# Preparing keys and values: context and integer weights transposed by the DMA engines, and a reordered opening

## The reference

```
k = (context @ Wk).reshape(B, Nk, h, dh)
v = (context @ Wv).reshape(B, Nk, h, dh)
attn = softmax(einsum('bqhd,bkhd->bhqk', q, k) * scale)
out  = einsum('bhqk,bkhd->bqhd', attn, v) @ Wo + bo

x = x + L0_xattn(layernorm(x), context, ...)
x = x + L0_ffn(layernorm(x), w_gate, w_up, w_down)     # int weights / 127
x = x + L1_xattn(layernorm(x), context, ...)
x = x + L1_ffn(layernorm(x), rhs)                      # quantised to int8
```

## Time and profile before

| | |
|---|---|
| median of three runs | 1627.0 us (1626.41 to 1629.02) |
| time of the profiled execution | 1625.34 us |
| span in its trace | 1623.5 us |
| TensorE busy | 1560.3 us (96%) |
| GpSimd busy | 1271.7 us (78%) |
| head | 0 to about 210.7 us |
| body | about 210.7 us to the end |

### The profile page before, as it was taken

One profiled execution on the slowest core, in us unless ns is written; L12 is line 12 of the kernel. 1 busy time (PEld: TensorE's weight loads), 2 busy tenths in 40 slices (PEclk: granted clock), 3 DMA queues, 4 the chain that ended last, 5 costly groups with the idle time before them and its releaser, 6 DMA issues.

```text
span 1623.5 us, 74775 instructions
## 1 busy us (share of the span) xinstructions
PE 1560.3 (96%) x27354; PEld 1446.7 (89%) x27354; DVE 1357.6 (84%) x3519; ACT 1379.5 (85%) x5665; POOL 1271.7 (78%) x1892
## 2 busy tenths in 40 slices
PE   7999978999999999999999999999999999999995
PEld 4555668999999999999999999999999999999994
DVE  5777757888888888888888887888898889888985
ACT  5665678899998998998999988889999999999993
POOL 4200068899999999998999888788999999999994
PEclk9999999999999999999999999999999999999998
DMA  8975689987887777778778989899999889989995
GB/s 253 327 275 223 221 183 175 160 176 173 176 177 178 168 174 182 166 177 176 171 172 179 173 172 161 153 178 197 191 201 198 189 190 200 198 190 190 196 191 104
DMA packets 732250, 305.82 MB, mean 188 GB/s; under 512 B 621424, under 2 KB 717584, under 8 KB 730064
## 3 DMA queue, kind: packets, MB, share of 16 engines
q1 hardware_dynamic: 730272, 297.29, 83.4%
q0 software_dynamic: 1840, 6.82, 1.3%
HBM read 87.72 MB, written 65.54 MB: 94 GB/s over the span
## 4 chain that ended last, share of the span: by engine, by line
PE 36%; POOL 31%; issue 11%; DVE 5%; DMA 2%; ACT 1%; SPq 1%; POOLq 0%; ACTq 0%; DVEq 0%
PE psum L308 27%; POOL pr L1486 9%; POOL p L1493 8%; POOL p L1489 6%; PE psum L1115 5%; POOL rs L368 3%; POOL hT_l L1476 3%; PE psum L306 2%; PE psum L299 2%; DVE oT_l L337 1%; DMA pT<-p 1%; DVE x L1465 1%; POOL y L1514 1%; POOL x_res L1502 1%; DMA x2T<-x 1%
## 5 line engine op out<-in xcount | busy, mean ns | idle before, releaser
L1230 ACT ACTIVATE ex<-psum,nmax 128x77 f32<-128x77 f32 x2048 | 638.0, 335 | 44.4 <-DVE nmax L1347 35.7
L1230 ACT ACTIVATION_READ_ACCUMULATOR ex<-psum,nmax 128x1 f32 x2048 | 443.3, 216 | 0.0
L1493 POOL TENSOR_TENSOR p<-pr,p 128x308 f16<-128x308 f32 x512 | 413.2, 807 | 38.4
L1486 POOL TENSOR_TENSOR pr<-ex,rden 128x308 f32<-128x308 f32 x512 | 369.8, 722 | 57.7 <-DVE rden L1352 57.1
L308 PE MATMUL psum<-xT,wq_h 128*64 128x256 f16 x4064 | 348.7, 273 | 0.0
L1347 DVE TENSOR_REDUCE nmax<-psum 128x4 f32<-128x308 f32 x512 | 241.1, 471 | 56.2 <-PE psum L308 53.8
L308 PE MATMUL psum<-xT,wq_l 128*64 128x256 f16 x2032 | 283.5, 273 | 0.0
L1489 POOL CAST p<-pr 128x308 f16<-128x308 f32 x512 | 242.3, 473 | 42.9 <-DMA pT<-p 10.7
L308 PE MATMUL psum<-kb,qT_h 128*64 128x154 f16 x4096 | 261.0, 231 | 11.5 <-DVE qT_l L340 4.1
L308 PE MATMUL psum<-wo_h,oT_h 128*64 128x256 f16 x1792 | 251.1, 275 | 15.2 <-DVE oT_l L337 14.5
L308 PE MATMUL psum<-wo_l,oT_h 128*64 128x256 f16 x1792 | 249.8, 273 | 0.0
(11 more groups left out here) (159 smaller groups left out, 3554.7 us busy)
## 6 DMA issues: line engine op xcount, KB each, us to landing
keys<-ks SPq DMA_DIRECT2D x16, 1232.0 KB, 5.2
kb<-keys SPq DMA_DIRECT2D x256, 77.0 KB, 2.8
vb<-vals SPq DMA_DIRECT2D x128, 154.0 KB
vals<-vs SPq DMA_DIRECT2D x64, 256.0 KB, 3.1
x_pair<-in_x_dram SPq DMA_DIRECT2D x32, 256.0 KB, 3.0
pT<-p SPq DMA_TRANSPOSE x512, 3.3
x_res<-in_x_dram SPq DMA_DIRECT2D x32, 256.0 KB, 3.0
mid_x<-y SPq DMA_DIRECT2D x32, 256.0 KB, 2.4
```

What stands on the lines that cost most here:

```text
L1230: last = act.activation(ex[i][:, t, b, :], SC[:, t, b * NK:(b + 1) * NK], ACT.Exp, bias=nmax[i][:, t, b:b + 1], accum_out=den[i][:, t, b:b ...
L1486: pool.tensor_tensor(pr[:, t, :, :], ex[i][:, t, :, :], r, ALU.mult).then_inc(s_p, 1)
L1493: pool.tensor_tensor(d[:, t, 1, :, 0:NK], pr[:, t, :, :], d[:, t, 0, :, 0:NK], ALU.subtract).then_inc(s_pl, 1)
```

## The change

Four things are altered, all in the head.

1. For group 0, each half is loaded as whole rows of 192 channels only; GpSimd copies channels 128 to 191 beside them. The first half is loaded ahead of the weights, and ScalarE and VectorE split it ahead of the weights too.
2. The first four key tiles are computed term by term: the first of the five products for all four banks, then the second, and so on, each with its own wait (`first_tiles`).
3. Groups 1 to 3 of the context are no longer turned by TensorE. The group is loaded in two transfers, split in its own layout by ScalarE and VectorE in two parts behind tiles 29 and 33, and transposed in float16 by one DMA transpose of 15 blocks of 128 x 128 on SP's queue, which stands between the two key stores of layer 1.
4. The integer weights are converted to float16 and transposed by DMA (36 blocks in all, in transposes of 3 or 6 blocks on SP's queue). TensorE waits for them ahead of the body.

The two splits of weights behind tiles 3 and 7 are moved behind tiles 5 and 9, and the second half of group 0 is split behind tile 3 and no longer behind tile 1.

```diff
-        WEIGHT_AT = {3: 2, 7: 3, 17: 4, 20: 5}
-        TURN_AT, SPLIT_AT = {29: 0, 37: 1}, {31: 0, 39: 1}
+        WEIGHT_AT = {5: 2, 9: 3, 17: 4, 20: 5}
+        WEIGHTS_AFTER = {(1, 0, 2): 0, (1, 0, 3): 1, (1, 1, 4): 2, (2, 0, 0): 3, (2, 0, 3): 5}
+        SPLIT_AT = {29: 0, 33: 1}
...
                 def load_half(n):
                     for (t0, rows), t in zip(SUB, range(3)):
                         src = ctx_t[n * HG + t0:n * HG + t0 + rows, :]
-                        sp.dma_start(cx[n % 2][0:rows, t, 0:DC], src).then_inc(s_cx[n % 2], 16)
-                        sp.dma_start(cx[n % 2][0:rows, t, DC:2 * P], src[:, P:DC]).then_inc(s_cx[n % 2], 16)
+                        sp.dma_start(cx[n][0:rows, t, 0:DC], src).then_inc(s_cx[n], 16)
...
+                def turn_group(g):
+
+                    sp.wait_ge(s_cgl, 2 * g)
+                    after(sp, s_kv, (g - 1) * KVT)
+                    sp.dma_start_transpose(ct[g % 2][:, :, :].rearrange("p r (t q) -> p (r t) q", q=P),
+                                           cx16[:, :, :, :].rearrange("p r t c -> p (r t c)")).then_inc(s_ctd, 16)
+
+                def turn_weights(j):
+
+                    sp.wait_ge(s_int, j + 1)
+                    dsts = turned[j][1]
+                    n = HID // len(dsts)
+                    for k, dst in enumerate(dsts):
+                        sp.dma_start_transpose(dst, w16[j % 4][:, k * n:(k + 1) * n]).then_inc(s_wd[j], 16)
...
+                load_half(0)
                 load_item(0)
                 load_item(1)
-                load_half(0)
                 load_half(1)
...
                             store_keys(i, l, half)
+                            if l == 1 and half == 0:
+                                turn_group(i + 1)
...
+                for n in range(2):
+                    pool.wait_ge(s_cx[n], 48)
+                    for rows, ts in ((P, slice(0, 2)), (SUB[2][1], slice(2, 3))):
+                        pool.tensor_copy(cx[n][0:rows, ts, DC:2 * P], cx[n][0:rows, ts, P:DC]).then_inc(s_cxd, 1)
...
+                def split_group(g, part):
+
+                    if part == 0:
+                        act.wait_ge(s_cg, 32 * g)
+                        after(act, s_ctd, 16 * (g - 1))
+                        act.activation(cx16[:, 0, :, :], cg[:, :, 0:P], ACT.Copy).then_inc(s_cgh, 1)
+                    else:
+                        act.activation(cx16[:, 2, :, 0:DCR], cg[:, :, P:DC], ACT.Copy).then_inc(s_cgh, 1)
...
+                split_half(0)
                 kv_high(0)
                 kv_high(1)
-                split_half(0)
-
-                def copy_turned(j):
-                    act.wait_ge(s_wt, j + 1)
...
+                def first_tiles():
+
+                    h0, l0, h1 = c0h[0][:, 0:HG], c0l[0][:, 0:HG], c1[0][:, 0:HG]
+                    for q, (w, r, s_need, need) in enumerate((
+                            (kf_h[0][0], h0, s_kh, 1), (kf_h[0][0], l0, s_cl, 1), (kf_l[0][0], h0, s_kl, 1),
+                            (kf_h[1][0], h1, s_kh, 2), (kf_l[1][0], h1, s_kl, 2))):
+                        pe.wait_ge(s_need, need)
+                        if q == 0:
+                            pe.wait_ge(s_ch, 1)
+                        if q == 3:
+                            pe.wait_ge(s_ch, 3)
+                            pe.wait_ge(s_cl, 2)
+                        for j in range(RING):
+                            last = pe.matmul(kv_bank(j, "k", j), w[:, j * P:(j + 1) * P], r, start=(q == 0),
+                                             stop=(q == 4))
+                            if q == 4:
+                                last.then_inc(s_kv, 1)
...
                     if l == 0 and kind == "k" and a == 0:
-                        pe.wait_ge(s_cl, 2 * (2 * i + b) + 2)
+                        if i == 0:
+                            pe.wait_ge(s_cl, 2 * b + 2)
+                        elif b == 0:
+                            pe.wait_ge(s_ctd, 16 * i)
...
                         if i == 0 and j == 3:
                             turn_half(1)
-                        if i < NG - 1 and j in TURN_AT:
-                            turn_half(2 * i + 2 + TURN_AT[j])
-                        if (i, j) in TURN_INT_AT:
-                            turn_ints(TURN_INT_AT[i, j])
```

More of the change, by code:

```diff
@@ L136, in xattn_ffn_kernel @@
         raw_f2 = sb("raw_f", [P, 2 * HID], F32, early)
-        raw_f = [raw_f2[:, i * HID:(i + 1) * HID] for i in range(2)]
+        raw_16 = raw_f2[:, :].bitcast(F16)
+        w16 = [raw_16[:, i * HID:(i + 1) * HID] for i in range(4)]
         r_amax = sb("r_amax", [P, KT], F32, early)
@@ L209, in xattn_ffn_kernel @@
         s_ct = sem("s_ct")
+        s_cxd = sem("s_cxd")
+        s_cg, s_cgh, s_cgl, s_ctd = sem("s_cg"), sem("s_cgh"), sem("s_cgl"), sem("s_ctd")
+        s_wd = [sem(f"s_wd{j}") for j in range(6)]
         s_ch = sem("s_ch")
@@ L400, in _ @@
                     if j == 5:
-                        for n in range(2, 4):
-                            sp.wait_ge(s_ct, 2 * n - 2)
-                            load_half(n)
+                        sp.wait_ge(s_ct, 4)
+                        load_group(1)
                 for l, bo in enumerate((bo0, bo1)):
@@ L566, in _ @@
                         high_tile(i, j, *tile)
[L567 removed]
+                        if i == 0 and j == 3:
                             split_half(1)
@@ L604, in split_half, with split_group @@
                                       ALU.subtract).then_inc(s_cl, 1)
+                def split_group(g, part):
+                    dve.wait_ge(s_cgh, 2 * (g - 1) + part + 1)
+                    if part == 0:
+                        low(dve, cx16[:, 1, :, :], cg[:, :, 0:P], cx16[:, 0, :, :]).then_inc(s_cgl, 1)
+                    else:
+                        low(dve, cx16[:, 2, :, DCR:P], cg[:, :, P:DC], cx16[:, 2, :, 0:DCR]).then_inc(s_cgl, 1)
                 def low_tile(i, j, l, kind, a, b):
@@ L610, in low_tile @@
                                              op1=ALU.subtract).then_inc(s_kvf, 1)
+                split_half(0)
                 kv_low(0)
                 kv_low(1)
-                split_half(0)
                 def convert(j):
                     dve.wait_ge(s_ri[j], 16)
-                    if j < 2:
+                    if j < 4:
                         dve.wait_ge(s_kp, 3)
                     else:
-                        dve.wait_ge(s_wt, j - 1)
-                    dve.tensor_copy(raw_f[j % 2], int_land[:, j, :]).then_inc(s_int, 1)
+                        dve.wait_ge(s_wd[j - 4], 16 * len(turned[j - 4][1]))
+                    o, i = w16[j % 4], int_land[:, j, :]
+                    if len(turned[j][1]) == KT:
+                        o = o.rearrange("p (k t q) -> p k t q", k=KT, q=P)
+                        i = i.rearrange("p (t k q) -> p k t q", k=KT, q=P)
+                        for k in range(KT):
+                            last = dve.tensor_copy(o[:, k], i[:, k])
+                    else:
+                        last = dve.tensor_copy(o, i)
+                    last.then_inc(s_int, 1)
                 def qo_low(k):
@@ L668, in _ @@
                         low_tile(i, j, *tile)
-                        if i == 0 and j == 1:
+                        if i == 0 and j == 3:
                             split_half(1)
@@ L753, in tile_product @@
                     last.then_inc(s_kv, 1)
[L755 to L762, removed]
                 def turn_rhs():
                     pe.wait_ge(s_rr, 16)
-                    pe.wait_ge(s_cl, 4 * NG)
+                    pe.wait_ge(s_cl, 4)
                     for t in range(KT):
@@ L1199, in body @@
                             gate_up(0, bank("gu", 0))
+                for j in range(NT):
+                    pe.wait_ge(s_wd[j], 16 * len(turned[j][1]))
                 bodies(pe, body, (1, 2))
```

56 lines of the change are left out of this document (28 added, 28 removed).

## The result

The changed kernel takes 1649.3 us (median of four, 1643.7 to 1653.5) beside 1626.7 us before: ratio 1.0135, interval 1.0103 to 1.0168. The profiled execution took 1643.7 us, its span is 1641.9. The mechanism of the change works, and yet 36 us are missing against the forecast of 1613.6 us: 26 of them in the body, which the change does not touch, and about 10 at the end of group 0.

A forecast was written before the change was run, and what follows sets the result against it. TensorE was taken to bound the kernel, 96% busy overall and 34.53 of 34.80 us in the head. The terms 3.7 + 6.4 + 4.1 + 0.6 - 1.4 = 13.4 us gave 1613.6 us, range 1610 to 1618.5.

The forecast's parts named there:

- The step that failed: Head to body: the body runs the same instructions, so a shorter head shortens the whole equally; no size of its own.
- rival D: Context transposes in the head: 15 blocks take far more than twice 8, making the kernel slower, for example 1645 us; chance 0.05.
- the wait for the turned context in group 0: Start of group 1: TensorE waits for the first DMA transpose, 1.4 us lost, up to 4.
- Rival B: From 41 to about 90 us DMA is the bound; late transpose, ScalarE waits for key stores; 1620.2 us, chance 0.17.
- The opening: Start of the head: the first value tile starts 3.7 us earlier, with bounds 2.0 and 4.5.
- Integers: Head: TensorE no longer turns the integer weights, six pieces, 4.1 us gained in all.
- Context halves and their stalls: Head: TensorE no longer turns six context halves, 6.4 us gained; fewer waits behind their splits, 0.6 us gained.
- A: Head: DMA queues share evenly, the transpose comes in time in all groups; gain 16.2 us, 1610.8 us; chance 0.14.

The follow-up runs named there:

- the 28: Changed kernel plus 28 do-nothing instructions spread over ScalarE's 208 head tiles, putting its first loop back in its old place: 1623.0 us (0.9966).
- moved loads: Changed kernel plus 28 do-nothing instructions, GpSimd loading the first query and output weights earlier, integer weights only after group 1's context is turned: 1612.5 us (0.9905).
- before with 228: Kernel before plus 228 do-nothing instructions spread over ScalarE's 208 head tiles: 1657.3 us (1.0175).
- 256: Kernel before plus 256 do-nothing instructions, a whole block, spread over ScalarE's 208 head tiles: 1627.0 us (1.0001).
- with 14: Changed kernel plus 14 do-nothing instructions on ScalarE, with GpSimd's weight loads moved as well: 1651.1 us, one execution.

## Why the prediction was wrong

**The step that failed** is this one: "The body begins when TensorE has finished the head, runs the same instructions as before [...]; a head shorter by G makes the whole shorter by G." The instructions are the same, but not their places: ScalarE's first loop starts 28 places earlier, in the band where each jump back waits for a fetch. That is 26.3 us here (with and without the 28), and it alone turns a gain into a loss. No part of the forecast's sum or rivals held it; rival D had the right sign, with another mechanism. What I could have seen: that the change takes 28 instructions out of a list ahead of a loop of 279. Whether the new place is a bad one the count alone doesn't say.

**A term that was mis-sized** is the wait for the turned context in group 0. I had 1.4 us with a bound of 4. In the traces it is 5.8 and 7.5 us, with ScalarE's waits for `qo_land` ahead of it, and its cure is worth 9.0 to 10.6 us. The rest of that is the half clock behind the wait, which the sum put at nothing: the body's first matmul starts 9.2 us later in the run with the 28 than in the one with moved loads too (205.77 against 196.60), 7.6 of it at tile 52 and 1.5 behind it. The sum treated the transpose as 3.3 us of work at the end of a queue of bytes. In the trace the 5 us from 45 us on moved 160 GB/s at a share of 1.20, where 256 GB/s passed before (a share above 1 means that the times of packets overlap):

```profile
45.00:50.00 5.00, 5.00 (x25) 2.16 (x23) 1.38 (x2) 1.51 (x3) 0.75 (x1) 1.00 1.20 160
```

Rival B had this place, a late transpose and ScalarE waiting, but had it wait for stores; it waited for loads. B priced it all at 8 us.

**The rest of the sum held.** The opening gained 5.1 us (3.7 forecast, bound 4.5). In the changed kernel's own trace the first product starts at 7.80 us, not 8.7, and the first value tile at 21.76, not 23.4. But one execution says little here: that tile starts at 21.76 to 24.05 us in the eight kernels with the new opening and at 27.39 to 29.39 in the four without it, and the 27.39 of the earlier trace rows, from which the term was taken, is the earliest of the four. Integers 2.9 (4.1). Context halves and their stalls 6.5 to 6.8 (6.4 + 0.6). In all 14.8 us with both faults cured, forecast 14.8 without the wait. That the two agree so closely is luck, the opening being 1.4 too low and the integers 1.2 too high; but each part is within 1.4 us, and the transpose by DMA does what was expected when it is not late. In that kernel tile 52 starts at 55.85 us, due in the forecast at 55.9, and the body's first matmul at 196.60 us, forecast 197; its time of 1612.5 us is 1.1 from the forecast. From before to after, by these runs: 1627.2 - 5.1 - 2.9 - 6.8 + 10.6 + 26.3 = 1649.3 us; it closes by its making, since the 6.8 of the context is what the other parts leave.

The evidence for A, an even share of the queues, is mixed. The transpose of group 0 was held up by the store ahead on its own queue and by the other queue together. What exactly in the two makes 23 us of 10 stays open; the experiments only show that either must be there.

## What to carry to other kernels

Count each engine's instructions ahead of a hardware loop, before and after a change, even of one that touches nothing in the loop. This loop of 279 instructions has starts at which it is fetched at every turn, and a longer one would have more of them by the same count. The mark is idle time by "issue" at the jump back and a rise of the instruction queue's packets, and a few instructions that do nothing move it out, at no cost that could be measured. The count gives how far the loop has moved; where the blocks end is read from the second wait or found by a run.

A transfer that an engine waits for goes ahead of a large store on the same queue when both become ready together; the order was worth 9 us here, and its price, a later store, was 1.07 us. And a gain is measured part by part: the whole change read as "slower" while each of its parts made the kernel faster.

## What the runs showed of the hardware that was not expected

- In the slow kernels ScalarE stands 2.25 to 3.17 us at a jump back, and the kernel is 26 to 39 us longer over 11 jumps (changed kernel with and without the 28: 26.3; before with 228 and 256: 30.3; with 14 and 28: 38.6, one execution). A second wait a few instructions on adds up to 0.55 us in the changed kernel, up to 1.53 in the one before with 228, and 1.72 to 2.85 in the one with 14. The first two start at the same place, so the place alone doesn't set the price; what else does is open.
- The issue of a DMA transpose of 15 blocks holds SP's queue for 1.57 to 12.19 us (group 0: 1.70 and 5.70 ahead of the key store, 7.58 to 12.19 behind it), and everything behind it on the queue waits as long.
- A TensorE that stands idle for 5.8 and 7.5 us goes on at half its clock: 1.3 and 1.5 us on top of the wait.
- 256 instructions that only increment a semaphore cost 208 tiles of ScalarE nothing (ratio 1.0001).
